# Float32 turns on TensorE: the transpose flag against an ordinary product with the identity

## The chip, the cores and the metric

One core of a Trainium2 chip runs the whole program. The metric is device time in microseconds (us), the median of several executions. TensorE (PE) works on two granted clocks, 1.2 and 2.4 GHz; the profile shows the granted share as 0.5 and 1.0.

## The reference, cut to what matters

The input is x, 6250 nodes by 256 channels, and 106,250 edges. A graph convolution gives four coefficients for each channel; they make the affine branch. Then a mixture of 16 experts (top 2) is applied to the normalised result, and both branches are added to x:

```
out = x[:, :, None] * coefs[None, :, :k] + coefs[None, :, k:]      # k = 2, x is the layer-normed input
x   = x + max(out, axis=-1)                                        # the affine branch
h   = relu(layernorm(x) @ w1[e] + b1[e]);  y = h @ w2[e] + b2[e]   # for the two experts that the gate picks
```

The coefficients belong to channels. Where a node lies on a partition, a channel lies along the free axis; to use a coefficient as a per-partition scalar the data must be turned, so that channels lie on the partitions, and turned back afterwards.

## The kernel before, in words

The program goes through four stages: the degrees and the weighted scatter of the edges (up to about 260 us of the profile's span), the affine branch with the gate and the routing (266 to 398 us), the expert tiles (398 to 815 us), and the gathering of the output.

The 49 tiles of 128 nodes are taken in 8 groups of 4, 5, 6, 7, 7, 7, 7 and 6 (`DG`). Each group but the first is split into two chunks of at most 4 tiles (`CH`, 15 chunks in all). Every chunk q takes this way through the engines:

- PE, `turn1(q)`, L1054: each 128x128 half of each tile of `XH` is turned into PSUM (`TA`, two buffers).
- ScalarE (ACT), `affine(q)`, L925: four activations read `TA` and write `bra` and `brb`, scale and bias being the channel's coefficients.
- VectorE (DVE), `widest(q)`, L1452: the larger of the two.
- PE, `back(q)`, L1186: the halves in `bra` are turned back into PSUM (`TB`, one buffer).
- DVE, `add_x(q)`, L1461 and L1464: adds x, writes `XH`, takes the statistics of the norm.

Behind it, for each group: ACT normalises (L950); PE turns the normalised tiles for the gate (`turn2`, L1201), ACT copies them (L946), PE multiplies by the gate's weights (`gate`, L1214, a 128x128 weight and 16 columns); DVE picks the top two (`route`), PE sums counts (`prefix`, L1226 and L1229), DVE gives slots (`place`, and once, after group 3, `fill_soon`), and GpSimd (POOL) scatters rows to `xs` by indirect DMA (L603). The order of PE's work is written out by hand; each engine works through its own list in order and waits on semaphores.

After the last `back`, SyncE waits for `returned` and `x_added` of all chunks and then loads the rows of the first expert tiles (L719). Expert tiles are float32 too: `up` (L1296) makes 8 ordinary products of a 128x128 weight and 128 columns for each of the 113 tiles, `down` (L1308) 4 products of 256 columns. At the end `y_sum` (L1334) adds pairs of rows by 98 ordinary float32 products with the identity as the weight. The counts named here for `turn1`, `back` and `turn2` (98 each), for `gate` (98 too: 49 tiles by 2 halves), `up` (904) and `y_sum` are calls in the source; a row of the profile counts instructions.

In L1054, L1186 and L1201 the data is the weight (the stationary operand) and the identity is what streams. In the profile PEld is the load of a weight, PE the product.

Of the kernel before, what the change touches and what calls it, by code (L numbers as in the profile page):

```python
# [14 lines left out]
P = 128  # L15
# [25 lines left out]
DG, _t = [], 0  # L41
# [37 lines left out]
def build(nc, x, src, dst, gW1, gb1, gW2, gb2, gate_w, gate_b, w1, b1, w2, b2, gamma, beta, out):  # L79
# [8 lines left out]
    with ctx:  # L88
        def sb(name, shape, dt):
            return ctx.enter_context(nc.sbuf_tensor(name, shape, dt))  # L90
# [12 lines left out]
        XH = sb("XH", [P, NT, C], fp32)  # L103
# [96 lines left out]
        bra = [bra0, bra1]  # L200
# [37 lines left out]
        ident = sb("ident", [P, P], fp32)  # L238
# [221 lines left out]
        TA = [PS[:, 2 * u:2 * u + 2, :].rearrange("p b c -> p (b c)").rearrange("p (j k m) -> p j k m", k=2, m=P) for u in range(2)]  # L460
        AT = [PS[:, 5, 2 * P:3 * P]] * (NDG - 1) + [PS[:, 7, 2 * P:3 * P]]
        TB = PS[:, 4:6, :].rearrange("p b c -> p (b c)").rearrange("p (t c) -> p t c", c=C)
# [28 lines left out]
        def y_sum(g, j):  # L491
            return PS[:, 4 * (g % 2) + j // 2, (j % 2) * C:(j % 2 + 1) * C]
# [27 lines left out]
        with nc.Block() as block:  # L520
# [526 lines left out]
            def _(pe):  # L1047
                def turn1(q):
                    g, j0, n = CH[q]
                    if q >= 2:  # L1050
                        pe.wait_ge(affined, q - 1)
                    for j in range(n):
                        for k in range(2):
                            last = nc.tensor.transpose(TA[q % 2][:, j, k, :], XH[:, DG[g][0] + j0 + j, k * P:(k + 1) * P], ident[:, :])  # L1054
                    last.then_inc(turned1, 1)

                pe.wait_ge(consts_set, N_CONSTS)
# [2 lines left out]
                for s, values in enumerate((dlo, da, db)):  # L1060
                    turned = PS[:, B_ROWS + s, :].bitcast(bf16).rearrange("p (b m) -> p b m", m=P)
                    for b in range(BLK):
                        cols = min(P, NCH - b * P)
                        last = nc.tensor.transpose(turned[0:cols, b, :], values[:, b * P:b * P + cols], identb[:, :])
                    last.then_inc(rows_turned, 1)

                for g in range(NG):
                    pe.wait_ge(deg_onehots, g + 1)
                    for c in range(GC):
                        last = nc.tensor.matmul(PS[0:HD, B_DEG, 0:LOD], oh_hi[g % 2][:, c // 2, :, c % 2],  # L1070
                                                oh_lo[g % 2][:, c // 2, 0:LOD, c % 2],
                                                start=(g == 0 and c == 0), stop=(g == NG - 1 and c == GC - 1))
# [32 lines left out]
                def scatter(n):  # L1105
                    g, i = n // 4, n % 4
                    if i == 0:
                        pe.wait_ge(weighted_ready, g + 1)
                    for c in range(8 * i, 8 * i + 8):
                        last = nc.tensor.matmul(PS[0:2 * NT, B_ACC, 0:P],  # L1110
                                                weighted[g % 2][:, c // 2, :, c % 2],
                                                oh_lo[g % 2][:, c // 2, :, c % 2],
                                                start=(n == 0 and c == 0), stop=(n == NSLOT - 1 and c == GC - 1))
                    if i == 3:
                        last.then_inc(scattered, 1)
                    return last
# [12 lines left out]
                for n in range(NSLOT - LAG, NSLOT):  # L1129
                    last = scatter(n)  # L1130
# [4 lines left out]
                                 start=True, stop=False)  # L1135
# [5 lines left out]
                for t in range(NT):  # L1141
                    q = 32 * (t % 4)
                    last = nc.tensor.matmul(PS[q:q + 1, 4, 0:C], wts[:, t:t + 1], XH[:, t, :], start=False, stop=False)
                nc.tensor.matmul(PS[:, 4, 0:C], zerob[:, :], zerob[:, :].unsqueeze(1).to_broadcast([P, 2, P]), start=False,
                                 stop=True).then_inc(v_done, 1)
                turn1(0)
                pe.wait_ge(v_rows_copied, 1)
                for k in range(2):
                    last = nc.tensor.matmul(PS[:, 2, k:k + 1], vrows[:, k * P:(k + 1) * P], ones1[:, :],
                                            start=True, stop=True)  # L1150
# [3 lines left out]
                for k in range(2):  # L1154
                    last = nc.tensor.matmul(PS[0:HID, 3, 0:1], gW1_sb[:, k, :], vcol[:, k:k + 1],
                                            start=(k == 0), stop=(k == 1))
# [3 lines left out]
                for k in range(2):  # L1160
                    for j in range(4):
                        at = (4 * k + j) * P
                        last = nc.tensor.matmul(PS[:, 3, 8 + 4 * k + j:9 + 4 * k + j], gW2_sb[:, at:at + P], th[:, :],
                                                start=True, stop=True)
# [6 lines left out]

                pe.wait_ge(z_ready, 1)
                turn1(1)

                issued = [0]

                def back(q):
                    g, j0, n = CH[q]
                    pe.wait_ge(maxed, q + 1)
                    if q >= 1:  # L1180
                        pe.wait_ge(x_added, q)
                    if issued[0]:
                        pe.wait_ge(prefix_read, issued[0])
                    for j in range(n):
                        for k in range(2):
                            last = nc.tensor.transpose(TB[:, j, k * P:(k + 1) * P], bra[q % 2][:, k, j, :], ident[:, :])  # L1186
                    last.then_inc(returned, 1)

                def turn2(g, b):
# [29 lines left out]
                def prefix(g):  # L1219
# [12 lines left out]
                    issued[0] = g + 1  # L1232

                back(0)
                turn1(GCH[1][1])
                back(GCH[1][0])
                turn1(GCH[2][0])
                turn2(0, 0)
                turn2(0, 1)
                gate(0, 0)  # L1240
                back(GCH[1][1])
                gate(0, 1)
                turn1(GCH[2][1])
# [83 lines left out]
                for g in range(NFG):  # L1327
# [4 lines left out]
                    for j in range(n):  # L1332
                        for k in range(2):
                            last = nc.tensor.matmul(y_sum(g, j), ident[:, :], y_two[g % YBUFS][:, j, k, :],  # L1334
                                                    start=(k == 0), stop=(k == 1))
# [462 lines left out]
```

## Time and profile before

| what | value |
|---|---|
| median of 3 runs | 889.9 us (886.05, 889.9, 895.62) |
| the profiled execution, span from first to last instruction | 882.4 us |
| what the median has beside that span | 7.5 us |
| mean granted clock of TensorE | 0.913 |
| PE busy | 741.0 us (84%) |
| DVE busy | 676.2 us (77%) |
| ACT busy | 475.4 us (54%) |

The profiled execution has no time of its own beside its span, so sums are made against the span, and 7.5 us are added to compare with the median. Ends of matmuls are modelled in the profile: a row of n matmuls lasts n-1 paces and the modelled length of the last one.

### The profile page before, as it was taken

To read this page: it belongs to the slowest core of one execution; us is meant where nothing else is said; L and a number is where in the kernel's file an instruction comes from. 1 tells how busy PE (TensorE), PEld (TensorE's weight loads), DVE (VectorE), ACT (ScalarE), POOL (GpSimd) and SP (SyncE) were. 2 spreads that over 40 slices of the span, in tenths; PEclk is the share of its full clock that TensorE was granted. 3 is DMA by queue.
4 is the path that set the end of the run, shared out by engine and by line. 5 is a ranking of instruction groups with operands and counts; after the bars stand their busy time and mean duration, and the time that the engine had idled before them with its cause. 6 is when DMAs were issued, how large, how long until landed. Compare 5 with 4: busy or idle time off the path is not lost.

```text
span 882.4 us, 21305 instructions
## 1 busy us (share of the span) xinstructions
PE 741.0 (84%) x6322; PEld 643.2 (73%) x6322; DVE 676.2 (77%) x1837; ACT 475.4 (54%) x1199; POOL 282.7 (32%) x313
## 2 busy tenths in 40 slices
PE   3555788888885776897899999999999999998893
PEld 3555355555555765876889999999998999997682
DVE  6999699999963688776757777777776777775597
ACT  5995677777635675653334444444444444443253
POOL 8400000000000457777734544544422222223010
PEclk9999699999997676568999999999999999999796
DMA  9850444445616944459999999899999999893999
GB/s 270 223 162 1 130 148 152 165 142 175 172 64 237 227 133 145 128 152 292 254 278 280 267 264 263 266 264 261 269 254 335 323 260 273 262 262 116 353 319 200
DMA packets 156240, 192.82 MB, mean 219 GB/s; under 512 B 78235, under 2 KB 125262, under 8 KB 153036
## 3 DMA queue, kind: packets, MB, share of 16 engines
q1 hardware_dynamic: 127048, 109.40, 44.7%
q10 hardware_dynamic: 15448, 51.04, 17.4%
q0 software_dynamic: 13632, 31.03, 11.2%
q8 instruction: 53, 0.87, 0.4%
q14 instruction: 59, 0.48, 0.2%
HBM read 151.05 MB, written 40.34 MB: 217 GB/s over the span
## 4 chain that ended last, share of the span: by engine, by line
PE 60%; DVE 23%; issue 8%; DMA 3%; ACT 3%; SPq 2%; DVEq 0%; ACTq 0%; POOL 0%; POOLq 0%
PE PS L1296 21%; PE PS L1308 19%; DVE W L1357 8%; PE PS L1334 4%; DVE W L1388 3%; DVE W L1423 3%; PE PS L1090 3%; PE PS L1186 2%; PE PS L1201 2%; DMA R<-xs 2%; PE PS L1214 2%; PE PS L1110 2%; SPq L719 2%; PE PS L1054 1%; DVE st L1464 1%
## 5 line engine op out<-in xcount | busy, mean ns | idle before, releaser
L1296 PEld LDWEIGHTS PS<-R,W 128*128 128x128 f32 x1808 | 223.1, 195 | 17.2 <-DVE R L1640 11.9
L1296 PE MATMUL PS<-R,W 128*128 128x128 f32 x1808 | 225.1, 278 | 9.7 <-DVE R L1640 9.7
L992 ACT ACTIVATE R<-PS,b1T 128x128 f32<-128x128 f32 x350 | 102.9, 367 | 233.9 <-PE PS L1296 233.8
L1308 PE MATMUL PS<-W,R 128*128 x904 | 213.9, 380 | 0.0
L610 POOL DMA_INDIRECT ys<-W,R x113 | 109.7, 971 | 230.9 <-DVE W L1692 228.5
L1308 PEld LDWEIGHTS PS<-W,R 128*128 128x128 f32 x904 | 163.6, 191 | 17.4
L1357 DVE TENSOR_TENSOR W<-R,W 128x3136 bf16<-128x3136 bf16 (+1 forms) x104 | 157.2, 1571 | 0.7 <-PE PS L1070 0.7
L890 ACT ACTIVATE W<-PS 128x1024 f16<-128x1024 f32 x104 | 106.2, 1023 | 38.0 <-PE PS L1090 32.0
L603 POOL DMA_INDIRECT xs<-W,slot_i x98 | 101.8, 1039 | 75.0 <-DVE slot_i L1522 46.3
L1090 PE MATMUL PS<-W,table 114*128 114x512 f16 x208 | 66.3, 403 | 26.3 <-DVE W L1388 25.9
L595 POOL MEMSET R<- 128x261 f32 x1 | 0.3, 317 | 226.4 <-PEq L1132 226.4
L1110 PE MATMUL PS<-W 128*98 128x128 bf16 x832 | 68.0, 226 | 2.2 <-DVE W L1423 2.2
L1070 PE MATMUL PS<-W 128*64 128x98 bf16 x832 | 44.3, 212 | 30.2 <-DVE W L1357 30.1
L1649 DVE TENSOR_SCALAR R<-PS,b1T 128x128 f32<-128x128 f32 x102 | 35.5, 348 | 43.3 <-PE PS L1296 42.5
L1070 PEld LDWEIGHTS PS<-W 128*64 128x64 bf16 x832 | 40.8, 113 | 33.5 <-DVE W L1357 33.5
L1101 PEld LDWEIGHTS PS<-sel,W 128*128 128x128 f16 x832 | 30.5, 97 | 43.3 <-ACT W L890 36.9
L1110 PEld LDWEIGHTS PS<-W 128*98 128x98 f16 x832 | 55.3, 128 | 2.4 <-DVE W L1423 2.4
L1334 PE MATMUL PS<-W,ident 128*128 128x256 f32 x196 | 47.5, 406 | 10.5 <-DMA W<-ys 7.3
L1001 ACT ACTIVATE gW_all<-R 128x256 f32<-128x256 f32 x113 | 56.1, 496 | 0.2
L1692 DVE SCALAR_TENSOR_TENSOR W<-PS,R,gW_all 128x256 f32<-128x256 f32 x113 | 53.8, 476 | 2.3 <-PE PS L1308 2.1
L1681 DVE SCALAR_TENSOR_TENSOR gW_all<-W,R,gW_all 128x256 f32<-128x256 f32 x113 | 53.8, 476 | 0.1
L1423 DVE TENSOR_TENSOR W<-W,R 128x1568 f16<-128x1568 bf16 x52 | 48.3, 971 | 6.1 <-ACT R L881 6.1
(264 smaller groups left out, 1028.9 us busy)
## 6 DMA issues: line engine op xcount, KB each, us to landing
W<-in_L_ffn_w ACTq DMA_DIRECT2D x96, 512.0 KB, 5.0
W<-key_rows SPq DMA_DIRECT2D x26, 784.0 KB
W<-in_L_ffn_w SPq DMA_DIRECT2D x33, 512.0 KB, 8.5
R<-xs SPq DMA_DIRECT2D x113, 130.5 KB
W<-ys SPq DMA_DIRECT2D x4, 2048.0 KB, 13.0
R<-xs SPq DMA_DIRECT2D x224, 32.0 KB
XH<-in_x SPq DMA_DIRECT2D x6, 896.0 KB, 11.7
W<-xs SPq DMA_DIRECT2D x116, 32.0 KB
```

The source lines that it names most:

```text
L603: nc.gpsimd.indirect_dma_start(out=xs[:, :], out_offset=bass.IndirectOffsetOnAxis(ap=slot_i[0:rows, g % XNBUFS, j, k:k + 1], axis=0), in_= ...
L610: nc.gpsimd.indirect_dma_start(out=ys[:, :], out_offset=bass.IndirectOffsetOnAxis(ap=home[:, h:h + 1], axis=0), in_=O3[o], in_offset=None) ...
L890: act.activation(masked[0:2 * HD, n % 3, :].rearrange("p (h m) -> p h m", h=2), PS[0:2 * HD, bank:bank + 2, :], ACT.Relu).then_inc(masked_ ...
L992: last = act.activation(HT3[:, u, j, :], up_out(u, j), ACT.Relu, bias=b1T[:, ds(e, 1), j])
L1070: last = nc.tensor.matmul(PS[0:HD, B_DEG, 0:LOD], oh_hi[g % 2][:, c // 2, :, c % 2], oh_lo[g % 2][:, c // 2, 0:LOD, c % 2], start=(g == 0 ...
L1090: last = nc.tensor.matmul(PS[0:2 * HD, B_R + 2 * (n % 2) + h, :], table[0:KT, :], oh_t[0:KT, g % 2, at:at + 4 * P], start=True, stop=True)
L1110: last = nc.tensor.matmul(PS[0:2 * NT, B_ACC, 0:P], weighted[g % 2][:, c // 2, :, c % 2], oh_lo[g % 2][:, c // 2, :, c % 2], start=(n == 0 ...
L1296: last = nc.tensor.matmul(up_out(u, j), W1S[b][:, k, j * P:(j + 1) * P], XT3[:, u, k, :], start=(k == 0), stop=(k == 1))
L1308: last = nc.tensor.matmul(PS[:, 6 * u, 0:C], HT3[:, u, j, :], wt2(e * W2COLS, j), start=(j == 0), stop=(j == 3))
L1334: last = nc.tensor.matmul(y_sum(g, j), ident[:, :], y_two[g % YBUFS][:, j, k, :], start=(k == 0), stop=(k == 1))
L1357: return nc.vector.tensor_tensor(into, pairs_of.to_broadcast([P, GC // 2, size, 2]), iota2[:, 0:size, :].unsqueeze(1).to_broadcast([P, GC ...
L1423: ins = nc.vector.tensor_tensor(weighted[u][:, :, k * NT:(k + 1) * NT, :], oh_hi[u][:, :, 0:NT, :], g16[:, u, k, :].rearrange("p (c r) -> ...
```

## The change

The instruction that turns is written as an ordinary matmul instead of a transpose, at two of three places. Operands, their roles, their order and the semaphores stay; the turns for the gate (`turn2`, L1201) and the small ones stay transposes.

```
 turn1:
-    last = nc.tensor.transpose(TA[q % 2][:, j, k, :], XH[:, DG[g][0] + j0 + j, k * P:(k + 1) * P], ident[:, :])
+    last = nc.tensor.matmul(TA[q % 2][:, j, k, :], XH[:, DG[g][0] + j0 + j, k * P:(k + 1) * P], ident[:, :],
+                            start=True, stop=True)
 back:
-    last = nc.tensor.transpose(TB[:, j, k * P:(k + 1) * P], bra[q % 2][:, k, j, :], ident[:, :])
+    last = nc.tensor.matmul(TB[:, j, k * P:(k + 1) * P], bra[q % 2][:, k, j, :], ident[:, :],
+                            start=True, stop=True)
```

## Rows read from the trace of the kernel before

**Rows 1.** The page: span, and the granted clock in 40 equal slices.

```profile
span 882.4 us, 21305 instructions
...
PEclk9999699999997676568999999999999999999796
```

**Rows 2.** Windows: length, busy us (count) PE, PEld, DVE, ACT, POOL, clock, DMA.

```profile
266.00:398.00 132.00, 98.91 (x575) 89.89 (x575) 93.02 (x410) 81.94 (x161) 72.26 (x69) 0.65 0.57 171
```

**Rows 3.** The chain of waits, 266 to 398 us: shares by line; pieces (start, length).

```profile
by line: PE PS L1186 14.8%; PE PS L1201 13.7%; PE PS L1214 12.8%; issue 8.1%; PE PS L1054 7.8%; DVE st L1464 6.2%; DVE XH L1461 6.1%; DVE R L1452 3.7%; DMA R<-xs 3.0%; SPq L719 2.4%; DVE mv L1470 2.4%; ACT W L925 2.2%; ACT R L925 2.0%; ACT 
...
275.86 1.98 PE PS L1186 x8
277.86 1.24 DVE XH L1461
```

**Rows 4.** Instructions by line: count, ns shortest/median/longest, first and last start.

```profile
L1054 PEld LDWEIGHTS PS<-ident,XH x98: 138/230/370, 266.0 to 361.4; 128*128 128x128 f32 x98
L1054 PE MATMUL PS<-ident,XH x98: 272/421/455, 266.1 to 361.6; 128*128 128x128 f32 x98
...
L1214 PE MATMUL PS<-gw_sb,W x196: 181/373/375, 286.1 to 396.3; 128*128 128x16 f32 x196
...
L1296 PEld LDWEIGHTS PS<-R,W x1808: 186/192/339, 397.9 to 808.9; 128*128 128x128 f32 x181
L1296 PE MATMUL PS<-R,W x1808: 272/275/580, 397.9 to 809.0; 128*128 128x128 f32 x181
```

**Rows 5.** Timeline of PE: start, length of the row, instructions (last xcount).

```profile
330.78 1.07 PE L1186 MATMUL PS<-ident,W 128*128 128x128 f32 x8 [0.45 <-issue]
351.58 1.94 PE L1186 MATMUL PS<-ident,W 128*128 128x128 f32 x8 [4.78 <-issue]
...
405.98 2.34 PE L1296 MATMUL PS<-R,W 128*128 128x128 f32 x10
411.00 1.28 PE L1296 MATMUL PS<-R,W 128*128 128x128 f32 x10
```

**Rows 6.** Timeline of PE and ACT: a group's last product, and its reader.

```profile
300.39 0.66 PE L1201 MATMUL PS<-ident,W 128*128 128x128 f32 x4 [0.69 <-ACT W L946]
301.09 0.60 ACT L946 ACTIVATE W<-PS 128x512 f32<-128x512 f32 x1 [0.27 <-PE PS L1201]
...
429.51 1.95 PE L1296 MATMUL PS<-R,W 128*128 128x128 f32 x16
431.60 1.14 ACT L992 ACTIVATE R<-PS,b1T 128x128 f32<-128x128 f32 x4 [1.79 <-PE PS L1296]
```

**Rows 7.** Windows of PE alone: length, busy (count), clock, DMA.

```profile
272.30:275.70 3.40, 0.00 (x0) 0.50 0.15 50
275.90:278.60 2.70, 2.70 (x13) 0.50 0.00 0
279.20:282.30 3.10, 0.51 (x5) 1.00 0.51 150
...
818.00:824.60 6.60, 4.55 (x10) 0.50 1.00 356
825.00:862.00 37.00, 36.91 (x172) 1.00 1.02 339
```

**Rows 8.** As Rows 2, 272 to 391.6 us: sums of full and half clock stretches.

```profile
306.20:316.50 10.30, 6.31 (x57) 5.64 (x55) 8.12 (x41) 8.57 (x17) 3.08 (x3) 1.00 0.41 130
326.80:337.00 10.20, 7.32 (x69) 6.80 (x67) 8.99 (x30) 7.99 (x17) 7.84 (x8) 1.00 0.44 139
sum 27.30, PE 17.05 PEld 15.49 DVE 20.74 ACT 21.63 POOL 13.48; mean PE 4.26 PEld 3.87 DVE 5.19 ACT 5.41 POOL 3.37
...
292.00:294.00 2.00, 0.10 (x1) 0.00 (x0) 1.72 (x18) 1.95 (x5) 0.00 (x0) 0.50 1.12 203
337.00:391.60 54.60, 45.40 (x219) 40.60 (x216) 43.00 (x213) 29.44 (x59) 41.85 (x41) 0.50 0.39 127
sum 92.30, PE 73.07 PEld 66.35 DVE 67.63 ACT 54.64 POOL 53.90; mean PE 14.61 PEld 13.27 DVE 13.53 ACT 10.93 POOL 10.78
```

## The prediction

> **What bounds the kernel now.** The page's first line and its clock row come first [rows 1]: the span is 882.4 us, and from the 13th to the 18th slice, which holds the changed lines, TensorE is granted 0.5 to 0.7 of its clock for most of the time. The window of that stage [rows 2] shows no engine full: 132.0 us, PE busy 98.9, DVE 93.0, ACT 81.9, mean clock 0.65. So the stage is bound by a chain that passes from engine to engine. The chain of waits for the same stretch [rows 3] gives the shares: `back` 14.8%, `turn1` 7.8%, `turn2` 13.7%, `gate` 12.8%. The two changed lines hold 22.6% of 132 us, 29.8 us of the chain; the two unchanged ones 26.5%, 35.0 us. A piece of `back` is followed at once by DVE's add [rows 3]: what makes `back` later makes the stage later. When the last `back` is done SyncE loads the first expert tiles, so the delay is handed on in full.
>
> **What one turn costs after the change.** The trace has no float32 product with a streamed identity here, but the ordinary float32 products beside it show the price [rows 4]. `turn1` is 98 calls and 98 instructions: a transpose is one load and one product. `gate` is 98 calls and 196 instructions; `up` is 113 tiles by 8, 904 calls, and 1808 instructions. An ordinary float32 product is thus two loads and two products. Their pace is that of a transpose [rows 5]: at half clock ten of `up` take 2.34 us, less a modelled last one of 0.42 that is 1.92/9 = 0.213 us, and eight of `back` (1.94-0.42)/7 = 0.217; at full clock (1.28-0.275)/9 = 0.112 against (1.07-0.272)/7 = 0.114. So each of the 196 changed turns goes from one pace to two, and 196 instructions are added.
>
> The Trainium skill ("Perfetto Trace Analysis", Transposes) says that turns should use the transpose and not an ordinary matmul, since it skips the arithmetic; the counts above agree. The Trainium skill ("TensorE: Matmul & The Clock Gate", Terms) calls the float32 transpose four times faster; the rows make it twice, and I go by them. By four, the sum below would be an estimated 40 us longer, two more times the changed lines' work of some 20 us at the clock forecast below.
>
> **Part 1, the doubled work with the clock as it was.** The 29.8 us on the chain are there twice: +29.8. Turns off the chain lie under DVE's add, statistics and maximum; at half clock, twelve gate instructions and six turns made double take 12 x 0.213 + 12 x 0.213 = 5.1 us, about what DVE needs, so no more than a few us come on top. This is the upper end.
>
> **Part 2, the clock.** Do the new products raise it? Both kinds did. After a stretch with nothing but transposes (275.9 to 278.6 us, PE busy without a break at 0.50) the clock is at 1.00 [rows 7]; in `y_sum`, ordinary float32 products, it is 0.50 while PE is busy 4.55 of 6.6 us and 1.00 once they come without a break [rows 7]. It is at half where PE waits: 272.3 to 275.7 us with nothing to do [rows 7], 292 to 294 with 0.10 us of work, and the wait of 4.78 us ahead of a `back` [rows 5, 8]. The gate's instructions stream 16 columns, keep PE busy by the profile, and yet the long stretch from 337 to 391.6 us, busy 45.4 of 54.6 with many of them, stays at half [rows 8].
>
> The change puts a second product of 128 columns beside each of 196, just at `turn1` and `back`, so the dense stretches become twice as long at half clock, and more often the clock should rise. At full clock the stage would be busy with (575 + 196) x 0.112 = 86 us of 132, 65%; the two long stretches that had full clock before were busy 6.31/10.3 = 61% and 7.32/10.2 = 72% [rows 2, 8]. So full clock at such a load is nothing new. I take it away from four places: the waits before 276, around 293 and 347 us, some 5 to 7 us each with the ramp behind them, and half of the 30 us after the last `turn1` at 361.6 [rows 4], where only `back` is denser. That is about 29 of 125 us: full clock in 0.77 of the stage's time.
>
> The other end is full clock throughout. By PE's busy time 73.07 of 90.12 us, 81%, was at half clock [rows 8]. Unchanged lines: 35.0 x 0.81 / 2 = 14.2 us saved. Changed lines: the 24.1 us at half clock are twice the work at twice the pace, so nothing; the 5.7 us at full clock double, +5.7. Together -8.5. From +29.8 at the old share of 0.19 to -8.5 at 1, 0.77, taken straight between them, gives 29.8 - 38.3 x 0.58/0.81 = **+2.4 us**. DVE lets this through: in the full-clock stretches it was busy 17.1 of 20.5 us, 83%, in the others 73% [rows 8], so what is late next is DVE, but only at the fast end.
>
> **Part 3, loads and results.** The load of an ordinary float32 weight is longer: 186 to 192 ns against 138 at full clock [rows 4]. It shows where PE was idle before, since the data to be turned is the weight: nine times on the chain, 9 x 0.05 = 0.5 us (0.9 at half clock). An ordinary group is read later: `turn2` ends at 301.05 and ACT starts at 301.09; `up` ends at 431.46 and ACT starts at 431.60 [rows 6]. That is 0.10 us more, on eight pieces of the chain that an engine follows: 0.8 (nothing, if the second semaphore that ACT waits for there makes it). Together **+1.2 us**, between 0 and 2. No semaphore wait is added. SyncE's loads move with the last `back`. POOL's scatters start when their slots are ready, and the expert stage needs the late ones only many tiles on, so they are costed at nothing; if POOL became late the tenth tile would wait.
>
> **The sum.** +2.4 + 1.2 = +3.6 on a span of 882.4 us: 886.0. The median of the runs lies 7.5 us above the profiled span, which gives 893.5; I say **893 us**.
>
> **Rivals.**
>
> *The clock does not follow (slower).* Place: `turn2`, `gate` and the waits lie between the dense pieces; if each dense piece comes to its end before the clock answers, the doubled products are paid at half clock. For: the dense piece at 316.5 to 326.8 us did not keep the clock, and 54.6 us in a row stayed at half [rows 8]. Against: twice the products. It decides where the share of full clock stays below 0.65: there the sum is 29.8 - 38.3 x 0.46/0.81 + 1.2 = +9.2, 1% of the time. At 0.5 it gives +16.3, **906 us**; with the old share 921 us. Chance 0.19.
>
> *Full clock nearly throughout (faster).* Then -8.5 + 1.2 = -7.3, 882.6, **883 us**, and 881 or less where the later loads and results of part 3 are hidden too. Against: the waits of PE at 272, 292 and 347 us, which the change does not remove, and DVE at 83%. The Trainium skill ("TensorE: Matmul & The Clock Gate", Part 4: PE-mode transpose) says that the transpose does not engage the full clock; by it, taking the flag off would give just this case. The trace disagrees: 13 transposes and nothing else stand ahead of a rise to 1.00 [rows 7]. Chance of this case 0.12, about half of it below 881 us.
>
> *The change costs no second instruction.* The identity might be streamed once as now; then only part 3 remains, 891 us. For: the shape is that of a transpose. Against: `y_sum` and `gate`, one with the identity and one with other weights, are both of the doubled kind. Chance 0.05.
>
> *Four instructions for a product.* Then the changed lines' work, 24.1 + 2 x 5.7 = 35.5 us at half clock and 17.8 at full, some 20 at the clock forecast, comes two more times, 893 + 40 = **933 us**; `gate` and `up`, with two each, speak against it [rows 4]. Chance 0.02.
>
> **How the numbers follow.** The forecast, 0.65 to 0.9 of the time at full clock, has 0.62. The runs of the kernel before lie from 886.05 to 895.62 us, 0.5% about their median; 1% (881.0 to 898.8) is about what can be told from no change. Forecast, single instruction and half of the faster rival lie within it but for 0.03 of the forecast that falls above: 0.62 + 0.05 + 0.06 - 0.03 = 0.70. Slower: 0.19 + 0.02 + 0.03 = 0.24. Faster: 0.06. The range runs from 884, a full clock with little hidden and the lower runs, to 905, the slower rival at a share of one half; below and above lies about 0.1 each. The likeliest case's own range is 887 to 899.
>
> **What would show it.** L1054 and L1186 with 196 instructions each and a load of about 190 ns at full clock show the doubling; 98 would refute it. The mean clock of the stage, 0.65 before, should come to 0.85 or more; below 0.75 the slower rival holds. `turn2` and `gate`, which are untouched, should lose about 10 us of their 35 on the chain, and the changed lines should hold 35 to 45 us of it. The start of the first `up`, 397.9 us before [rows 4], should move by less than 5 us, and everything behind it in step. If the stage grew in windows with the clock at 1.00, neither the clock nor the count would be the cause, and the forecast's working would be wrong.

## The result, and the profile after

The changed kernel took 905.0 us (median of 4 runs, 899.0 to 910.4) beside 888.0 us, a ratio of 1.016 (95%: 1.011 to 1.020). Run once more for a narrower interval it took 902.8 us beside 891.3, 1.010 (1.006 to 1.013). The ratios with their intervals, here and below, are not the quotients of the medians, which are 1.019 and 1.013. So by the ratios the change costs 1.0 to 1.6%, some 9 to 14 us; the medians lie 17.0 and 11.5 us apart. The forecast was 893 us, with a chance of 0.70 for a time that cannot be told from no change. The time came out at the very end of the range, 905 us, where the slower rival stood, and both intervals lie above 1.

The page of the changed kernel, first line and clock row (compare [rows 1]):

```profile
span 899.0 us, 21697 instructions
...
PEclk9999699999998798756999999999999999999797
```

There are 392 instructions more, 196 products and 196 loads, and the clock in the slices of the stage is higher. The lines of the two places (as [rows 4]):

```profile
L1054 PEld LDWEIGHTS PS<-ident,XH x196: 186/192/338, 266.2 to 371.4; 128*128 128x128 f32 x196
...
L1187 PE MATMUL PS<-ident,W x116: 275/421/582, 277.0 to 396.6; 128*128 128x128 f32 x116
...
L1187 PE MATMUL PS<-ident,R x80: 274/276/581, 284.4 to 386.3; 128*128 128x128 f32 x80
```

Each of 98 calls is now two instructions, as those of `up` and `gate` were. The stage from the first `turn1` to the first `up`, in windows (columns as in [rows 2]): the whole, the sum of six stretches at full clock, two of the seven stretches at half, and the sum of these seven:

```profile
266.00:410.40 144.40, 109.49 (x771) 103.19 (x769) 92.78 (x410) 82.15 (x161) 74.33 (x72) 0.80 0.52 159
...
sum 71.50, PE 53.45 PEld 50.71 DVE 52.59 ACT 48.78 POOL 31.05; mean PE 8.91 PEld 8.45 DVE 8.77 ACT 8.13 POOL 5.18
...
354.80:368.40 13.60, 8.73 (x41) 8.76 (x42) 9.95 (x37) 3.82 (x9) 10.26 (x12) 0.51 0.41 132
382.00:402.50 20.50, 18.07 (x82) 15.62 (x83) 14.16 (x84) 8.05 (x19) 15.63 (x17) 0.51 0.33 106
...
sum 58.10, PE 45.34 PEld 42.62 DVE 35.02 ACT 27.57 POOL 37.20; mean PE 6.48 PEld 6.09 DVE 5.00 ACT 3.94 POOL 5.31
```

132.0 us became 144.4: 12.4 of the 16.6 us by which the span grew. The other 4.2 us lie outside the stage; over the profiled executions of all kernels here what lies outside took from 750.4 to 759.9 us, so they are not put down to the change. The clock did rise, from 0.65 to 0.80, and unlike before the stretches from 310 to 355 us are at full but for 3.4 us. But 58 us stayed at half, and there the doubled turns are paid in full. The last stretch of 20.5 us holds the last turns back, on which SyncE waits.

One turn back at each clock, in the timelines of PE and DVE (start, length, instructions), and the last one with the add behind it:

```profile
338.98 2.02 PE L1187 MATMUL PS<-ident,W 128*128 128x128 f32 x16 [0.45 <-issue]
341.12 1.22 DVE L1463 TENSOR_TENSOR XH<-PS,W 128x1024 f32<-128x1024 f32 x1 [1.12 <-PE PS L1187]
...
359.67 3.75 PE L1187 MATMUL PS<-ident,W 128*128 128x128 f32 x16 [6.90 <-issue]
363.54 1.22 DVE L1463 TENSOR_TENSOR XH<-PS,W 128x1024 f32<-128x1024 f32 x1 [2.85 <-PE PS L1187]
...
397.17 0.96 DVE L1463 TENSOR_TENSOR XH<-PS,W 128x768 f32<-128x768 f32 x1 [3.31 <-PE PS L1187]
```

Four tiles turned back take 2.02 us at full clock and 3.75 at half; with the flag it was 1.94 at half [rows 5]. So a doubled group at full clock costs what a single one cost at half, and one at half costs 1.8 us more. The clock fell in the 6.90 us of waiting ahead of the slow one, in which DVE writes the routing tables: it is 1.00 up to 354 us and 0.50 from 356.

A trap in the chain of waits after the change: by line it gives POOL's scatters 11.7%:

```profile
by line: PE PS L1187 15.8%; issue 12.3%; POOL xs L603 11.7%; PE PS L1054 9.7%; PE PS L1203 5.9%; PE PS L1216 5.7%; DVE st L1466 4.7%; DVE XH L1463 4.1%; DMA R<-xs 3.1%; DVE R L1454 2.8%; SPq L719 2.2%; ACT W L925 2.0%; ACT R L925 1.9%; DVE 
```

SyncE's wait is for scatters of groups 1 to 3 and for the last add. POOL had begun the 44 scatters of groups 0 to 3 by 374.5 us (windows of line L603):

```profile
290.00:374.50 84.50, 47.08 (x44) 0.84 0.53 153
374.50:397.50 23.00, 17.39 (x18) 0.60 0.28 100
```

The eighteen on the chain belong to later groups, and one of their landings only happens to lie beside the end of the last add, 397.17 + 0.96 = 398.13 us; SyncE goes on at 398.20 and issues its first loads (L719) from 398.92. By the waits in the source the chain really runs back through that add.

### The profile page after: what moved, and what is told of

Its sections match the earlier page's. It is cut to its first block, busy times and chain, and to the rows that moved or that the text cites. A ratio compares the mean times of both kernels' runs of the same rounds, so it can differ in the third digit from the quotient of the medians.

```text
span 899.0 us, 21697 instructions
## 1 busy us (share of the span) xinstructions
PE 754.3 (84%) x6518; PEld 656.9 (73%) x6518; DVE 674.4 (75%) x1837; ACT 475.8 (53%) x1199; POOL 282.0 (31%) x313
## 4 chain that ended last, share of the span: by engine, by line
PE 51%; DVE 25%; issue 10%; DMA 5%; SPq 4%; ACT 2%; POOL 2%; DVEq 0%; ACTq 0%; POOLq 0%
PE PS L1298 19%; PE PS L1310 17%; DVE W L1359 9%; PE PS L1336 4%; DVE W L1425 4%; DMA R<-xs 4%; DVE W L1390 3%; SPq L719 3%; PE PS L1187 3%; POOL xs L603 2%; PE PS L1054 2%; PE PS L1091 2%; PE PS L1203 1%; PE PS L1111 1%; PE PS L1216 1%
## 5 line engine op out<-in xcount | busy, mean ns | idle before, releaser
L1298 PEld LDWEIGHTS PS<-R,W 128*128 128x128 f32 x1808 | 221.8, 194 | 22.0 <-DVE R L1642 16.8
L603 POOL DMA_INDIRECT xs<-W,slot_i x98 | 100.7, 1027 | 84.3 <-DVE slot_i L1524 55.7
L1336 PE MATMUL PS<-W,ident 128*128 128x256 f32 x196 | 48.4, 412 | 10.3 <-DMA W<-ys 7.1
L1336 PEld LDWEIGHTS PS<-W,ident 128*128 128x128 f32 x196 | 40.2, 207 | 18.2 <-DMA W<-ys 8.2
```

The lines of the kernel that those rows point to most:

```text
L603: nc.gpsimd.indirect_dma_start(out=xs[:, :], out_offset=bass.IndirectOffsetOnAxis(ap=slot_i[0:rows, g % XNBUFS, j, k:k + 1], axis=0), in_= ...
L1298: last = nc.tensor.matmul(up_out(u, j), W1S[b][:, k, j * P:(j + 1) * P], XT3[:, u, k, :], start=(k == 0), stop=(k == 1))
```

## The experiments

All ratios are against the kernel before, on the same chip; windows are each from the first `turn1` to the first `up` of one profiled execution.

**Back alone.** Only the turns back lose the flag.

```
 turn1:  nc.tensor.transpose(TA[...], XH[...], ident[:, :])             # as before
 back:   nc.tensor.matmul(TB[...], bra[...], ident[:, :], start=True, stop=True)
```

> Only the 15 groups of turns back (L1186) are ordinary products; turn1 keeps the flag. Theory 'count': an ordinary float32 product is two instructions, and nearly every turn back lies on the chain, so most of the loss of the full change (+14 us, 1.016) comes from here: +7 to +14 us, L1186 with 196 instructions, L1054 with 98, stage clock between 0.65 and 0.80. Rival 'clock': the loss came from where full clock was missed, and with half the added products it is missed more often: +14 us or more. Rival 'load': only the longer weight load at starts from idle counts: +1 us.

Measured: 1.011 (1.005 to 1.018), 903.8 us. The profiled execution took 908.4 us, the four 897.9 to 908.4:

```profile
266.30:413.10 146.80, 109.34 (x671) 102.59 (x671) 93.26 (x409) 81.97 (x161) 70.97 (x70) 0.69 0.51 155
```

98 more products cost as much as the 196 of the full change, with the clock hardly raised, 0.69. On the chain `back` has 26.8% of the 146.8 us, 39.3 us, twice the 19.5 of before [rows 3]. That is "count"; for "load" it is far too much. "Clock" asked for 14 us or more, 1.016, which lies just inside the interval, and the medians lie 14.3 us apart; this run alone does not exclude it.

**Turn in alone.** Only `turn1` loses the flag.

```
 turn1:  nc.tensor.matmul(TA[...], XH[...], ident[:, :], start=True, stop=True)
 back:   nc.tensor.transpose(TB[...], bra[...], ident[:, :])            # as before
```

> Only turn1 (L1054) is made of ordinary products; the turns back keep the flag. Theory 'count': turn1 lies partly under DVE's work, 7.8% of the chain of 132 us: +2 to +7 us, or about nothing if the denser turn1 raises the clock for turn2 and gate behind it. Rival 'clock': with half the added products full clock is missed more often than in the full change: +10 us or more. Rival 'load': 0 to +1 us.

Measured: 1.000 (0.997 to 1.004). The stage, and its chain of waits:

```profile
264.70:395.40 130.70, 97.99 (x671) 90.76 (x670) 92.85 (x410) 81.83 (x161) 69.11 (x67) 0.76 0.56 170
...
by line: PE PS L1054 14.3%; PE PS L1187 11.7%; PE PS L1215 11.6%; PE PS L1202 10.8%; issue 9.9%; DVE XH L1462 5.3%; DVE st L1465 5.2%; DMA R<-xs 3.3%; DVE R L1453 3.1%; ACT W L950 2.5%; SPq L719 2.5%; PE PS L1164 2.3%; ACT W L925 2.2%; ACT 
```

98 more products at `turn1` cost nothing, and the clock is 0.76. They are not hidden beside DVE's work: `turn1` holds 14.3% of 130.7 us of the chain, 18.7 us, where it held 10.3 [rows 3]. But `back`, `gate` and `turn2` (here L1187, L1215 and L1202) fell from 54.5 us to 44.6. So the denser work pays for itself through the clock, which is the lowest end of what "count" allowed. "Clock", 10 us or more, falls.

**The flag, twice.** Every turn keeps the transpose flag and is issued twice, the second over the first.

```
+    for _ in range(2):
         last = nc.tensor.transpose(TA[...], XH[...], ident[:, :])      # and likewise in back
```

> Every turn in and turn back keeps the transpose flag and is issued twice, the second over the first; so the count of instructions is that of the full change, without an ordinary product. Theory 'count': the same as the full change, +10 to +18 us (1.011 to 1.020), stage clock about 0.80, since a flagged turn raises the clock like an ordinary product. Rival 'flag' (transposes do not engage the full clock): the clock of the stage stays at 0.65 or falls, and the doubled work is paid at half clock: +25 us or more. Rival 'load' (the price is the longer load of an ordinary float32 weight): +5 us or less.

Measured: 1.010 (1.007 to 1.013). A line of its loads, and the stage:

```profile
L1055 PEld LDWEIGHTS PS<-ident,XH x196: 138/140/370, 264.8 to 366.7; 128*128 128x128 f32 x196
...
264.90:405.40 140.50, 105.06 (x769) 99.30 (x769) 93.41 (x409) 82.25 (x161) 73.53 (x72) 0.82 0.54 164
```

Without one ordinary product among the turns in and back, the time is that of the full change, 1.010 to 1.016, and the clock is raised as there (0.82 beside 0.80), though the loads are short, 138 ns. So the price is the number of instructions, as far as these intervals tell, and a flagged turn raises the clock as an ordinary product does. "Flag" (0.65 or less, 25 us) and "load" (5 us or less) fall.

**The changed kernel again.** No edit.

> The changed kernel itself, for a narrower interval beside the others. If the flagged turn issued twice (1.010) is the whole of the loss: 1.008 to 1.013. If the ordinary product costs more than two flagged turns (longer load of each weight): 1.014 or more.

Measured: 1.010 (1.006 to 1.013). The stage of its profiled execution:

```profile
265.10:412.70 147.60, 112.48 (x769) 106.47 (x768) 93.37 (x410) 82.44 (x161) 73.82 (x72) 0.78 0.52 156
```

Beside the flag twice this leaves nothing for the longer loads, within 0.5%. The first ratio, 1.016, taken alone would be the other case; why it lies higher is not explained, and the two intervals overlap from 1.011 to 1.013. With both together up to some 0.6% may be the ordinary product's own. The stages of single executions, 144.4 and 147.6 us here and 140.5 with the flag twice, cannot settle it, since two of the same kernel lie 3.2 us apart.

**Fillers, flag kept.** The kernel before, with products of zeros in PE's waits.

```
+def fill(count):
+    for _ in range(count):
+        nc.tensor.matmul(PS[:, 6, 0:P], zerob[:, :], zerob[:, :], start=True, stop=True)
...
 turn1(1)
+fill(34)
...
+fill(24)
 prefix(0)
+fill(16)
 back(GCH[2][0])
...
+    fill(40 if g == 6 else 24 if g == 4 else 10)
     back(GCH[g + 1][0])
+    if g == 2: fill(24)
     turn2(g, 0)
...
+    if g == 4: pe.wait_ge(turned2_read, T2[g + 1]); fill(80)
     back(GCH[g + 1][1])
```

> The kernel before, with small bf16 products of zeros into an unread PSUM bank where PE waits in this stage (34, 24, 16, 10 or 24 or 40, 80 of 128 columns), so that PE has work in its waits; no turn is changed. If the half clock is what the stage pays for, it gets faster: stage clock 0.85 or more, 10 to 20 us less (0.98 to 0.99), since 52 us of the chain's PE work was at half clock. If DVE, ACT and POOL hold the stage whatever the clock, no change within 4 us; if the fillers stand in the way of turns that are ready, slower.

Measured: 0.993 (0.989 to 0.996), 884.5 us. The stage, and a stretch behind the 80 fillers:

```profile
264.10:388.20 124.10, 102.03 (x845) 93.90 (x844) 92.64 (x410) 81.45 (x161) 67.82 (x67) 0.80 0.59 180
...
345.80:366.20 20.40, 19.94 (x116) 19.17 (x116) 16.41 (x70) 13.35 (x26) 15.52 (x17) 0.51 0.40 137
```

Half clock is indeed what the stage pays for: with no turn touched it is 7.9 us shorter at 0.80. The clock did not come to the 0.85 expected, nor the gain to 10 us: the 80 fillers had run out 2.45 us ahead of the long wait's end, and the 20 us behind it ran at half.

**Fillers, changed kernel.** The same fillers in the kernel of the change.

> The changed kernel with the fillers of e5_flag_filled (products of zeros where PE waits). Theory 'count and clock': the changed kernel pays for its doubled turns where the clock is at half, so with a stage clock of 0.88 or more it comes back by 6 to 12 us, to within 0.5% of the kernel before, and stays 8 us or more behind e5_flag_filled, since on the chain two products are still two. Rival 'something else in the ordinary product' (load, later result): it stays 10 us or more above the kernel before whatever the clock.

Measured: 1.000 (0.997 to 1.003), 892.5 us.

```profile
267.80:400.30 132.50, 114.57 (x1041) 107.38 (x1040) 92.70 (x410) 81.77 (x161) 71.62 (x68) 0.91 0.54 162
```

At 0.91 the stage takes 132.5 us, as before the change at 0.65, and the loss is gone. It stays behind the same fillers with the flag, by 8.0 us between the medians and 0.7% between the ratios, at the edge of the 8 us or more expected: the clock made up for the second product and did not remove it.

**More fillers, flag kept.** As above, with 36 behind the third `turn1`, 116 in place of 80, others a little longer, and 28 and 44 at the first two expert tiles.

> The kernel before with more fillers: also behind the turn in of the third chunk, a longer one ahead of the turn back that waits for the routing tables (116), and at the first two expert tiles. Where e5 still ran 20 us in a row at half clock, this should hold it: stage clock 0.88 or more and 8 to 16 us less than the kernel before (0.982 to 0.991). If DVE and ACT already hold the stage at e5's clock: the same as e5, 0.993.

Measured: 0.988 (0.984 to 0.992), 882.4 us, the lowest median here; its interval overlaps that of the fillers before. Its profiled execution took 886.6 us. The stage, and a wait of ACT near its end:

```profile
264.80:394.70 129.90, 110.79 (x978) 103.34 (x978) 94.80 (x432) 81.56 (x161) 73.12 (x70) 0.80 0.62 183
...
381.80 0.21 ACT L939 ACTIVATE W<-tokc 128x6 f32<-128x6 f32 x1 [2.55 <-DMA xs<-W,slot_i]
```

The time is within what was expected, the clock of 0.88 is not met in this execution, so where its further gain lies is not shown. What stands in its way next is: ACT's normalising of the last group waits 2.55 us until POOL's scatters of the rows that it writes over have landed, and on the chain the 28 fillers stand directly ahead of the first `up`, for 2.96 us.

**The gate's turns too.** `turn2` also as an ordinary product, on top of the change.

```
-    nc.tensor.transpose(PS[:, 6, ...], xn[...], ident[:, :])
+    nc.tensor.matmul(PS[:, 6, ...], xn[...], ident[:, :], start=True, stop=True)
```

> The turns for the gate are ordinary products too, the third place, which the change left out. Theory 'count and clock': 98 more instructions on a part that holds 13.7% of the chain; as with turn1 alone the denser work raises the clock, but ACT waits for each group of turn2, so 0 to +8 us over the changed kernel. If clock were all, it would be faster than the changed kernel by 4 us or more.

Measured: 1.016 (1.011 to 1.020), 906.7 us.

```profile
264.70:411.40 146.70, 113.17 (x867) 108.39 (x866) 92.93 (x410) 82.35 (x161) 69.99 (x69) 0.87 0.51 154
```

The clock goes up to 0.87, and still it is no faster than the changed kernel; by the ratios 0 to 0.6% slower. Here the risen clock does not make up for instructions on the chain.

## Why the prediction was right and wrong

*The count was right.* Two instructions for an ordinary product, one for a flagged turn, read from calls against counts; their pace held too, (2.02-0.275)/15 = 0.116 us at full and (3.75-0.42)/15 = 0.222 at half. The flag issued twice shows that this is the price, to within some 0.5%. The estimate of 40 us more, from the float32 transpose as four times faster in the Trainium skill ("TensorE: Matmul & The Clock Gate", Terms), is not borne out.

*The direction of the clock was right, its extent was the step that failed.* The forecast took full clock in 0.77 of the stage; the windows of after give 71.5 of 129.6 us, 0.55. Put into the prediction's own line, 29.8 - 38.3 x (0.55 - 0.19)/0.81 = 12.8 us, and 14.0 with part 3; the stage grew by 12.4. (The 0.19 is a share of PE's busy time and the 0.77 one of time; by busy time after has 53.45 of 98.79 us, 0.54, so mixing them does little here.) So the sum was sized well and the share was not. It was the slower rival's case, which had 0.19: below its border of 0.65, near its point of 0.5 with 906 us. That the time still lay within the range is owed to the room made for this rival, not to the forecast.

Of the four places given away two came as foreseen: 272.9 to 279.7 and 296.7 to 303.6 us, 6.8 and 6.9 us at half. The wait at 353 us cost 13.6 us at half and not 5 to 7, since the doubled turn back behind it ran at half all through; and of the part without `turn1`, where 15 us were allotted, 24.0 us were at half (3.5 from 375.2 us, and 20.5 on end). Two short stretches, at 307 and 331 us, 3.4 each, were not foreseen: the first begins with a turn back behind a run of `gate`, the second in a turn back behind a wait of 2.28 us.

*The claim that the flag keeps the clock down was refuted as forecast.* The Trainium skill ("TensorE: Matmul & The Clock Gate", Part 4: PE-mode transpose) says so; flagged turns issued twice had a stage clock of 0.82 against 0.65 with them once. The rule of the Trainium skill ("Perfetto Trace Analysis", Transposes) to use the transpose stands: giving it up cost 1.0 to 1.6%.

*Part 3 was too much.* DVE starts 0.12 us after the last product of a turn back at either clock (341.00 and 341.12, 363.42 and 363.54), as before (331.85 and 331.96 for the group in [rows 5]). So the 0.10 us read from `up` and ACT [rows 6] is not the product's. Longer loads exist, 186 to 192 ns, but the comparison with the flag twice leaves them no cost that stands clear of the intervals.

*The base was misread, without harm.* The runs of after lie 1.7 us above their spans (900.73 and 899.0), so most of the 7.5 us between the median and the profiled span of before was that execution being a quick one, not time around it. The forecast's time is the same either way, 889.9 + 3.6.

*The tests named.* 196 instructions each, with loads of about 190 ns at full clock: met. Clock of 0.85 or more: 0.80, in between the two bounds named. The first `up` was to move by less than 5 us and moved from 397.9 to 410.4. The shares on the chain, 35 to 45 us for the changed lines and some 25 for `turn2` and `gate`, come to 36.8 and 16.8 us by the line above, but that chain runs over POOL from 374.9 us on, so they are not to be read.

## What to carry to other kernels

Compare calls in the source with instructions in the profile before an operation is exchanged for another that "does the same": a float32 product was two where the flagged turn was one. What an added instruction costs depends on its place and on what it does to the clock: 98 of them at `back`, where the next engine waits, cost 1.1% at a stage clock of 0.69, and 98 at `turn1` nothing at 0.76. Where a stage runs at half clock because its engine waits, cheap work in the waits gave more (0.993 and 0.988) than any form of the useful work tried here.

## What the runs showed of the hardware that was not expected

Products of zeros in bf16, 10 to 116 at a time in PE's waits, brought the stage from 0.65 to 0.80, and in the changed kernel from 0.80 to 0.91. And the clock can be bought with the doubled work itself: `turn1` alone as an ordinary product took the stage from 0.65 to 0.76 and paid for its own 98 instructions to within 0.4%. Turns with the flag raise it too: issued twice, they took it to 0.82.
